# Code search on one Trainium2 core: the add of the chosen codes as an accumulating DMA, four buffers for the gathered rows, a later store

## The chip, the cores and the metric

The kernel runs on one core of a Trainium2 chip. The metric is the device time of one execution in microseconds; less is better. Engines are named PE (matrix), PEld (its weight loads), DVE (vector), ACT (scalar), POOL (GpSimd) and SP (the engine that only issues DMAs); "POOLq" and "SPq" are their sequencers.

## The reference

The input x is (8, 64, 256, 256) in float32. Two layers are added to it, each on a group-normalised copy (32 groups, so two channels to a group):

```
x = x + dct_conv(gn(x), weights1, weights2)   # cosine transform, 64x64 mix of 2 x 32 x 32 modes, transform back
x = x + nearest_code(gn(x), embeddings)       # rows of D = 64 values, K = 1024 codes
def nearest_code(x, e):
    flat = x.reshape(-1, 64)
    distances = sum(flat^2) + sum(e^2) - 2 * flat @ e
    return e.T[argmin(distances, axis=1)]      # the chosen code itself
```

## The kernel before, in words

The work is cut into 256 groups (`NG`), each two channels of one image, kept as a tile `X[:, buf8]` of 128 partitions by 1024 floats, eight of them in turn. The first 0.8 ms of the kernel do the forward transform of all groups (stage A) and the mixing of modes (stage M); both use tiles `Xb` and `Oc`, which nobody touches afterwards. The change is in stage B, which fills the rest: for each group it transforms back and adds x, normalises, searches the best code for each row of 64 values, and adds that code.

A group holds 131072 values, so 2048 rows of 64, and these are 16 steps (`NT`) of 128 rows, one row to a partition. Codes are scored in pairs: in each step PE makes two 128x512 results, the score of the even code and the difference to the odd one (L554), ACT takes the positive part of the difference (`relu`, L723), and DVE adds the two and keeps the maximum (`best`, L929), then finds its place (`find`, L939), which is the number of the pair. POOL then gathers by an indirect DMA (`gather`, L1033) the 128 rows of the pair table: 196 floats each, with both codes, their difference and the difference of their norms. A group later DVE decides between even and odd from the gathered rows: `products` in two halves (L948, at step 5 and 6 of the next group), `sum_products` (L953), ACT's `sum_product`, `choose` (L959, step 13), `settle` in two halves (L964, step 14 and 15). Then `finish` (L1040) on POOL adds the chosen code into X, and SP stores X (`store_y`).

All engines run their own program, in order; the order is written out by hand. Groups are unrolled by eight (`U`), in a loop of 32 passes; each engine branches at the end of a pass. Of POOL's program this is what one group asks: gathers of step 0 to 15, with `inverse_deviation(three)` (L1026) after the gather of step 13, and `finish(before)`, the add of the previous group, after the gather of step 15. Since the gather of step 15 waits for a `find` that runs in step 0 of the next group, the add runs at the start of the next group but one.

The gathered rows lie in `q`, which has two buffers; the gather of step 0 waits until `finish` of two groups before is done (`b_fin`). `best` and `find` have four buffers in flight, and `find` of step 0 waits until the gathers of two groups before have landed.

SP's program for each group r is: turn the normalised halves of group r + 1 by a transposing DMA (`turn_y`) and copy them when they have landed (`copy_yh`), half 0, then half 1; load X of group r + 5 (`load_x`); load its modes (`load_modes`); then store group r - 1 (`store_y`), which waits for `b_fin`.

Of the kernel before, what the change touches and what calls it, by code (L numbers as in the profile page):

```python
# [28 lines left out]
ALU = mybir.AluOpType  # L29
# [8 lines left out]
P = 128  # L38
# [3 lines left out]
U = 8  # L42
NI = NG // U
# [10 lines left out]
D = 64  # L54
K = 1024
NP = K // 2
NT = CG * H * W // D // P
ROW = 3 * D + 4
TA = 8
LOW = (3, 7)  # L60
HT = (slice(0, NT // 2), slice(NT // 2, NT))
# [52 lines left out]
def need(eng, sem, count):  # L114

    if not isinstance(count, int) or count > 0:
        eng.wait_ge(sem, count)


def program(nc, x, w1, w2, emb, c_fh, c_fw, c_ih, c_iw, c_id, c_gm, c_rm, out):  # L120
    spec = nc.dram_tensor("spec", [B, C, MX * MY], F32, kind="Internal").ap()
    mixed = nc.dram_tensor("mixed", [NG, MX, CG * MY], F32, kind="Internal").ap()
    table = nc.dram_tensor("table", [NP, ROW], F32, kind="Internal").ap()
# [8 lines left out]
    with ExitStack() as ctx:  # L132
        def sb(name, shape, dt=F32):
            return ctx.enter_context(nc.sbuf_tensor(name, shape, dt))

        def sem(name):
            return ctx.enter_context(nc.semaphore(name))
# [30 lines left out]
        sc = sb("sc", [P, 9])  # L168
# [23 lines left out]
        def from_arena(*dims):  # L192

            size = int(np.prod(dims))
            taken[0] += size
            assert taken[0] <= 2 * C * CH
            names = "abc"[:len(dims)]
            return arena[:, taken[0] - size:taken[0]].rearrange(
                f"p ({' '.join(names)}) -> p {' '.join(names)}", **dict(zip(names, dims)))

        Xc = sb("Xc", [P, 2, B, CH])
        Xb = sb("Xb", [P, 2, CH, 2 * B])
        Oc = sb("Oc", [P, 2, C, MY])
# [9 lines left out]
        Y = from_arena(4, NT, D)  # L213
# [3 lines left out]
        Fm = from_arena(4, NP)  # L217
        mx = sb("mx", [P, 4])
        idx = sb("idx", [P, 2, NT, 8], U32)
        q = from_arena(2, NT, ROW)  # L220
        prod = from_arena(NT, D)
        dot = sb("dot", [P, NT])
        odd = sb("odd", [P, NT], I32)
# [28 lines left out]
        gath = [sem(f"gath{n}") for n in range(4)]  # L252
        b_inv, b_t, b_conv, b_x1, b_sq, b_st, b_delta2, b_ve, b_rs, b_rr, b_nb = (
            sem("b_" + n) for n in "inv t conv x1 sq st delta2 ve rs rr nb".split())
        b_y, b_yl, b_sc, b_rl, b_ttr, b_mi, b_p, b_red, b_dot, b_sel, b_pr, b_fin = (
            sem("b_" + n) for n in "y yl sc rl ttr mi p red dot sel pr fin".split())
        b_ls = sem("b_ls")
        turned = [[sem(f"turned{h}{n}") for n in range(2)] for h in range(2)]
        t2_in = [[sem(f"t2_in{h}{n}") for n in range(2)] for h in range(2)]
# [1 line left out]
        def hold(eng, name, count):  # L261


            if not isinstance(count, int):
                eng.sem_inc(held[name], 1)
# [5 lines left out]
        def _(sp):  # L271
# [67 lines left out]
            def load_x(g):  # L339
                need(sp, y_out[g.buf8], 16 * g.visit(8))  # L340
                sp.dma_start(X[:, g.buf8].rearrange("p (i f) -> p i f", i=CG), x_g[g.n]).then_inc(x_in[g.buf8], 16)

            def load_modes(g):
                need(sp, b_inv, g.n - 1)
                sp.dma_start(M[:, g.buf2], mixed[g.n]).then_inc(m_in[g.buf2], 16)

            def store_y(g):
                need(sp, b_fin, g.n + 1)
                sp.dma_start(out_g[g.n], X[:, g.buf8].rearrange("p (i f) -> p i f", i=CG)).then_inc(y_out[g.buf8], 16)

            sp.wait_ge(a_h, NG // 2)
# [8 lines left out]
            def turn_y(g, h):  # L360

                need(sp, b_yl, 2 * g.n + h + 1)
                hold(sp, "sp", g.n)
                if h == 0:
                    need(sp, b_sc, NT * (g.n - 1))
                    hold(sp, "sp", g.n)
                sp.dma_start_transpose(t1[:, g.buf2, HT[h]],
                                       YS[:, HT[h]].rearrange("p k f -> p (k f)")).then_inc(turned[h][g.buf2], 16)

            def copy_yh(g, h):  # L370
                need(sp, turned[h][g.buf2], 16 * (g.visit(2) + 1))
                hold(sp, "sp", g.n)
                sp.dma_start(t2[0:D, g.buf2, HT[h]], t1[0:D, g.buf2, HT[h]]).then_inc(t2_in[h][g.buf2], 16)
# [7 lines left out]
            def body(i):  # L381
                for r in range(U):
                    if Group(i, r + 1).exists():
                        for h in range(2):
                            turn_y(Group(i, r + 1), h)
                            copy_yh(Group(i, r + 1), h)
                    if Group(i, r + 5).exists():
                        load_x(Group(i, r + 5))
                    if Group(i, r + 5).exists():
                        load_modes(Group(i, r + 5))  # L390
                    if Group(i, r - 1).exists():
                        store_y(Group(i, r - 1))

            body(0)
            with sp.Fori(1, NI - 1) as i:
                body(i)
            body(NI - 1)
            store_y(Group(NI - 1, U - 1))
            for n in range(U):
                sp.wait_ge(y_out[n], 16 * NI)  # L400

# [378 lines left out]
        def _(dve):  # L780
# [8 lines left out]
            V = nc.vector  # L789
# [152 lines left out]
            def products(g, h):  # L942
                if h == 0:
                    need(dve, gath[g.buf4], 16 * NT * (g.visit(4) + 1))
                else:
                    need(dve, b_dot, TA * g.n)
                hold(dve, "dve", g.n)
                V.tensor_tensor(prod[:, HT[h]], q[:, g.buf2, HT[h], 2 * D:3 * D], Y[:, g.buf4, HT[h]],  # L948
                                ALU.mult).then_inc(b_p, 1)

            def sum_products(g):
# [3 lines left out]
            def choose(g):  # L955
                need(dve, b_red, g.n + 1)
                need(dve, b_dot, TA * (g.n + 1))
                hold(dve, "dve", g.n)
                V.tensor_tensor(odd[:], dot[:], q[:, g.buf2, :, 3 * D], ALU.is_gt).then_inc(b_sel, 1)  # L959

            def settle(g, h):
                need(dve, b_sel, g.n + 1)
                hold(dve, "dve", g.n)
                V.copy_predicated(q[:, g.buf2, HT[h], 0:D], odd[:, HT[h]].unsqueeze(2).broadcast_to([P, NT // 2, D]),  # L964
                                  q[:, g.buf2, HT[h], D:2 * D]).then_inc(b_pr, 1)

            def small_step(g, k, at):

# [37 lines left out]
            for h in range(2):  # L1006
                products(last, h)
            sum_products(last)
            choose(last)
            for h in range(2):  # L1010
                settle(last, h)


        @block.gpsimd
        def _(pool):
            G = nc.gpsimd
            pool.wait_ge(amax_in, 1)
            G.partition_all_reduce(amax, amax0, P, RMAX).then_inc(amax_all, 1)
            pool.wait_ge(s_ve, 1)
            G.tensor_tensor(r_c[:], v_c[:], mhalf[:], ALU.pow).then_inc(s_rstd, 1)  # L1020


            def inverse_deviation(g):
                need(pool, b_ve, g.n + 1)
                need(pool, b_rr, g.n)
                G.tensor_tensor(rs, ve, mhalf[:, 0:1], ALU.pow).then_inc(b_rs, 1)  # L1026

            def gather(g, k):
                need(pool, b_mi, NT * g.n + k + 1)
                if k == 0:  # L1030
                    need(pool, b_fin, g.n - 1)
                hold(pool, "pool", g.n)
                G.indirect_dma_start(out=q[:, g.buf2, k], out_offset=None, in_=table,  # L1033
                                     in_offset=bass.IndirectOffsetOnAxis(ap=idx[:, g.buf2, k, 0:1], axis=0)
                                     ).then_inc(gath[g.buf4], 16)

            def finish(g):
                need(pool, b_pr, 2 * (g.n + 1))
                xg = X[:, g.buf8].rearrange("p (k d) -> p k d", d=D)
                G.tensor_tensor(xg, xg, q[:, g.buf2, :, 0:D], ALU.add).then_inc(b_fin, 1)  # L1040

            def body_b(i):
                for r in range(U):
                    g, before = Group(i, r), Group(i, r - 1)
                    three = Group(i, r + 3)
                    for k in range(NT):
                        gather(g, k)
                        if three.exists() and k == 13:
                            inverse_deviation(three)
                        if before.exists() and k == 15:  # L1050
                            finish(before)

            pool.wait_ge(tab_out, 16)
            inverse_deviation(Group(0, 0))
            inverse_deviation(Group(0, 1))
            inverse_deviation(Group(0, 2))
            body_b(0)
            with pool.Fori(1, NI - 1) as i:
                body_b(i)
            body_b(NI - 1)  # L1060
            finish(Group(NI - 1, U - 1))


# [30 lines left out]
```

## Time and profile before

| | us |
|---|---|
| median of 3 runs (7206.6 to 7208.57) | 7208.31 |
| the profiled execution's own time | 7212.89 |
| span of that execution, first to last instruction | 7210.9 |
| mean granted TensorE clock | 0.956 of full speed |

The times are of whole executions. The profile is of one execution, 4.6 us slower than the median, 2.0 us of which lie outside its span. In the page, the share of an engine is its busy time by the span; issuing a DMA counts as busy on POOL, where it takes POOL's own time, and not on SP. "Idle before" is what an engine waited, with the instruction or DMA that ended the wait; "issue" means that the profile shows no wait for anything.

### The profile page before, as it was taken

Reading aid. Unit: us, or ns where it says so; the run is one execution under the profiler, and the core shown is the slowest. Engines: PE = TensorE matmul, PEld = TensorE weight load, DVE = VectorE, ACT = ScalarE, POOL = GpSimd, SP = SyncE. Lnnn points to the kernel's source line nnn. Section 1 sums busy time; section 2 is a strip of 40 time slices with the busy share of each in tenths; the row PEclk is TensorE's granted clock in tenths of the full one; section 3 lists DMA queues with packets and bytes.
Section 4 is the critical chain, followed back from the end, with each engine's and each line's share of the span. In section 5 each row is a group of like instructions: output and inputs, shape, how many; then the busy total and the mean of one; then the engine's idle time right before and its main releaser. Section 6 shows DMA issues by size and latency. Waiting matters only on the chain. (4 is left out here: it accounts for less than half of the span.)

```text
span 7210.9 us, 142512 instructions
## 1 busy us (share of the span) xinstructions
PE 6465.4 (90%) x25616; PEld 2543.4 (35%) x25616; DVE 6512.0 (90%) x19053; ACT 4720.0 (65%) x12193; POOL 4800.5 (67%) x4614
## 2 busy tenths in 40 slices
PE   7898899999999999899998998998989999899997
PEld 3458333333333333333333333333333333333332
DVE  7771599999999999999999999999999999999998
ACT  2331576677767766667777776767767776777675
POOL 0000377777777777777777777777777777777777
PEclk9998899999999999999999999999999999999999
DMA  7989365665656555656656665556666665666565
GB/s 249 303 279 186 82 144 134 137 144 139 141 137 141 142 137 137 141 136 142 143 139 139 141 142 138 142 138 142 140 141 142 141 140 136 141 141 141 137 140 120
DMA packets 1139144, 1077.66 MB, mean 149 GB/s; under 512 B 702944, under 2 KB 843040, under 8 KB 1138144
## 3 DMA queue, kind: packets, MB, share of 16 engines
q1 hardware_dynamic: 924640, 651.61, 36.0%
q0 software_dynamic: 196608, 411.30, 25.6%
q14 instruction: 712, 5.83, 0.3%
q10 hardware_dynamic: 16896, 4.20, 0.3%
q8 instruction: 288, 4.72, 0.3%
HBM read 722.32 MB, written 143.01 MB: 120 GB/s over the span
## 5 line engine op out<-in xcount | busy, mean ns | idle before, releaser
L1033 POOL DMA_INDIRECT arena<-table,idx x4096 | 4042.6, 987 | 1592.2 <-issue 1157.6
L723 ACT ACTIVATE arena<-bank 128x512 f32<-128x512 f32 x4096 | 2435.0, 595 | 1673.4 <-PE bank L554 1503.9
L554 PE MATMUL bank<-eh,t 128*128 128x512 f16 x8192 | 2516.2, 389 | 576.9 <-DVE mx L929 342.4
L929 DVE CUSTOM_DVE_ANT_0 arena<-bank,arena 128x512 f32<-128x512 f32 x4096 | 2775.4, 678 | 265.6 <-ACT arena L723 217.0
L939 DVE FIND_INDEX8 idx<-mx,arena 128x8 uint32<-128x512 f32 x4096 | 2812.4, 687 | 0.0
L554 PE MATMUL bank<-el,t 67*128 67x512 f16 x8192 | 2504.1, 387 | 0.0
L554 PEld LDWEIGHTS bank<-eh,t 128*128 128x128 f16 x8192 | 590.9, 98 | 2534.1 <-issue 1407.6
L554 PEld LDWEIGHTS bank<-el,t 67*128 67x128 f16 x8192 | 817.4, 100 | 1013.1 <-issue 72.8
L1040 POOL TENSOR_TENSOR X<-X,arena 128x1024 f32<-128x1024 f32 x256 | 605.4, 2365 | 11.1 <-DVE arena L964 5.0
L519 PE MATMUL conv<-iw,Ts 64*128 64x512 f32 x1024 | 586.1, 653 | 0.0
L514 PE MATMUL conv<-X,ident 128*128 128x512 f32 x1024 | 556.4, 625 | 2.4 <-issue 1.8
L533 PE MATMUL bank<-arena,ident 128*128 128x512 f32 x1024 | 550.6, 619 | 6.0 <-ACT arena L703 4.6
L711 ACT ACTIVATE arena<-arena 128x64 f32<-128x64 f32 x2048 | 499.9, 248 | 13.4 <-DVE arena L948 13.4
L855 DVE BATCH_NORM_STATS2 st<-X 128x6 f32<-128x512 f32 x512 | 324.1, 679 | 97.0 <-DMA X<-x 90.9
L948 DVE TENSOR_TENSOR arena<-arena 128x512 f32<-128x512 f32 x512 | 359.3, 702 | 54.4 <-DMA arena<-table,idx 52.5
L711 ACT ACTIVATION_READ_ACCUMULATOR arena<-arena 128x1 f32 x2048 | 397.4, 194 | 0.0
L717 ACT CAST YS<-bank 128x512 f16<-128x512 f32 x512 | 299.6, 585 | 138.5 <-PE bank L534 137.8
L964 DVE COPY_PREDICATED arena<-odd,arena 128x512 f32<-128x512 int32 x512 | 374.9, 733 | 0.0
L939 DVE MATCH_VALUE_LOAD idx<-mx,arena 128x8 f32 x4096 | 354.7, 87 | 0.0
L929 DVE DVE_READ_ACCUMULATOR2_ANT mx<- 128x1 f32 x4096 | 346.3, 85 | 0.0
L1020 POOL TENSOR_TENSOR r_c<-v_c,mhalf 128x8 f32<-128x8 f32 x1 | 1.7, 1692 | 508.9 <-DVE v_c L889 508.9
L1026 POOL TENSOR_TENSOR small<-small,mhalf 128x1 f32<-128x1 f32 x256 | 148.7, 581 | 273.5 <-DVE small L921 269.1
(107 smaller groups left out, 4565.9 us busy)
## 6 DMA issues: line engine op xcount, KB each, us to landing
X<-x SPq DMA_DIRECT2D x512, 512.0 KB, 4.4
y<-X SPq DMA_DIRECT2D x256, 512.0 KB, 3.1
t<-t SPq DMA_DIRECT2D x512, 128.0 KB
arena<-table,idx POOLq DMA_INDIRECT x4096
arena<-w SPq DMA_DIRECT2D x12, 2048.0 KB, 23.0
arena<-w SPq DMA_DIRECT2D x64, 128.0 KB, 3.0
t<-YS SPq DMA_TRANSPOSE x512
spec<-Fs SPq DMA_DIRECT2D x256, 16.0 KB, 3.5
```

The source lines that it names most:

```text
L514: nc.tensor.matmul(conv[:, t].rearrange("p (i w) -> p i w", i=CG), ident[:], xg[:, t], start=True, stop=False)
L519: nc.tensor.matmul(conv[:, t], Ts[:, t * P:(t + 1) * P], iw[:], start=False, stop=True).then_inc(b_conv, 1)
L533: nc.tensor.matmul(low, ident[:], Y[:, g.buf4, HT[h]], start=True, stop=False)
L554: last = nc.tensor.matmul(bank[4 + place(k) % 2 if e else k % 4][:], tile[0:rows, g.buf2, k], codes[0:rows, e], start=rows == P, stop=rows ...
L711: nc.scalar.activation(prod[:, k], prod[:, k], ACT.Identity, accum_out=dot[:, k:k + 1]).then_inc(b_dot, 1)
L723: nc.scalar.activation(R[:, k % 4], bank[4 + place(k) % 2][:], ACT.Relu).then_inc(b_rl, 1)
L929: V.tensor_tensor_reduce(out=Fm[:, k % 4], in0=bank[k % 4][:], in1=R[:, k % 4], scale=1.0, scalar=-3.0e38, op0=ALU.add, op1=ALU.max, accum ...
L939: V.max_index(idx[:, g.buf2, k], mx[:, k % 4:k % 4 + 1].broadcast_to([P, 8]), Fm[:, k % 4]).then_inc(b_mi, 1)
L948: V.tensor_tensor(prod[:, HT[h]], q[:, g.buf2, HT[h], 2 * D:3 * D], Y[:, g.buf4, HT[h]], ALU.mult).then_inc(b_p, 1)
L964: V.copy_predicated(q[:, g.buf2, HT[h], 0:D], odd[:, HT[h]].unsqueeze(2).broadcast_to([P, NT // 2, D]), q[:, g.buf2, HT[h], D:2 * D]).then ...
L1033: G.indirect_dma_start(out=q[:, g.buf2, k], out_offset=None, in_=table, in_offset=bass.IndirectOffsetOnAxis(ap=idx[:, g.buf2, k, 0:1], axis=0)
L1040: G.tensor_tensor(xg, xg, q[:, g.buf2, :, 0:D], ALU.add).then_inc(b_fin, 1)
```

## The change

Three things change. `finish` on POOL becomes a DMA with `accum_op=ALU.add`, issued by POOL, that reads the first 64 floats of each of the 16 gathered rows of a partition (16 runs of 256 bytes) and adds them into the partition's 4096 bytes of X. Its landing raises `b_fin[buf4]` by 16. The gathered rows get four buffers: two as before, and one each in the tiles `Xb` and `Oc`; the gather of step 0 now waits for the add of four groups before. SP's store moves from the end of group r's list, where it stored group r - 1, to a place behind the turned halves and ahead of `load_x`, where it stores group r - 2.

```
-        q = from_arena(2, NT, ROW)
+        q = [from_arena(NT, ROW) for n in range(2)]
+        for kept in (Xb[:].rearrange("p v m b -> p (v m b)"), Oc[:].rearrange("p v o m -> p (v o m)")):
+            q.append(kept[:, 0:NT * ROW].rearrange("p (k w) -> p k w", k=NT))
...
+        b_fin = [sem(f"b_fin{n}") for n in range(4)]
...
             def store_y(g):
-                need(sp, b_fin, g.n + 1)
+                need(sp, b_fin[g.buf4], 16 * (g.visit(4) + 1))
...
                         for h in range(2):
                             turn_y(Group(i, r + 1), h)
                             copy_yh(Group(i, r + 1), h)
+                    if Group(i, r - 2).exists():
+                        store_y(Group(i, r - 2))
                     if Group(i, r + 5).exists():
                         load_x(Group(i, r + 5))
                     if Group(i, r + 5).exists():
                         load_modes(Group(i, r + 5))
-                    if Group(i, r - 1).exists():
-                        store_y(Group(i, r - 1))
...
-            store_y(Group(NI - 1, U - 1))
+            for r in range(U - 2, U):
+                store_y(Group(NI - 1, r))
...
             def gather(g, k):
                 need(pool, b_mi, NT * g.n + k + 1)
                 if k == 0:
-                    need(pool, b_fin, g.n - 1)
+                    need(pool, b_fin[g.buf4], 16 * g.visit(4))
                 hold(pool, "pool", g.n)
-                G.indirect_dma_start(out=q[:, g.buf2, k], out_offset=None, in_=table,
+                G.indirect_dma_start(out=q[g.buf4][:, k], out_offset=None, in_=table,
...
             def finish(g):
                 need(pool, b_pr, 2 * (g.n + 1))
+                hold(pool, "pool", g.n)
                 xg = X[:, g.buf8].rearrange("p (k d) -> p k d", d=D)
-                G.tensor_tensor(xg, xg, q[:, g.buf2, :, 0:D], ALU.add).then_inc(b_fin, 1)
+                G.dma_start(xg, q[g.buf4][:, :, 0:D], accum_op=ALU.add).then_inc(b_fin[g.buf4], 16)
```

`products`, `choose` and `settle` read the same rows under the new name `q[g.buf4]`.

## Rows read from the trace of the kernel before

**Rows 1.** The page, its first lines: the span, and each engine's busy time.
```profile
span 7210.9 us, 142512 instructions
...
PE 6465.4 (90%) x25616; PEld 2543.4 (35%) x25616; DVE 6512.0 (90%) x19053; ACT 4720.0 (65%) x12193; POOL 4800.5 (67%) x4614
```

**Rows 2.** The page's groups: line, engine, operation, count | busy us, mean ns | idle before.
```profile
L1033 POOL DMA_INDIRECT arena<-table,idx x4096 | 4042.6, 987 | 1592.2 <-issue 1157.6
...
L929 DVE CUSTOM_DVE_ANT_0 arena<-bank,arena 128x512 f32<-128x512 f32 x4096 | 2775.4, 678 | 265.6 <-ACT arena L723 217.0
L939 DVE FIND_INDEX8 idx<-mx,arena 128x8 uint32<-128x512 f32 x4096 | 2812.4, 687 | 0.0
...
L1040 POOL TENSOR_TENSOR X<-X,arena 128x1024 f32<-128x1024 f32 x256 | 605.4, 2365 | 11.1 <-DVE arena L964 5.0
...
L948 DVE TENSOR_TENSOR arena<-arena 128x512 f32<-128x512 f32 x512 | 359.3, 702 | 54.4 <-DMA arena<-table,idx 52.5
```

**Rows 3.** Windows: length, then busy us of each engine, granted clock, DMA share, GB/s.
```profile
3841.80:3865.40 23.60, 22.30 (x84) 8.16 (x83) 23.60 (x73) 17.68 (x47) 17.37 (x17) 1.00 0.54 142
3937.30:3961.30 24.00, 22.12 (x83) 8.10 (x82) 23.76 (x73) 17.67 (x47) 18.69 (x18) 1.00 0.70 146
3801.60:4001.10 199.50, 180.82 (x656) 65.97 (x656) 190.17 (x568) 141.29 (x369) 148.00 (x143) 0.97 0.59 140
```

**Rows 4.** Timeline of POOL about one group: start us, duration us, [idle before].
```profile
3912.28 0.96 POOL L1033 DMA_INDIRECT arena<-table,idx  x1 [0.80 <-issue]
...
3930.08 0.58 POOL L1026 TENSOR_TENSOR small<-small,mhalf 128x1 f32<-128x1 f32 x1
...
3932.13 0.95 POOL L1033 DMA_INDIRECT arena<-table,idx  x1 [0.30 <-issue]
3933.10 2.37 POOL L1040 TENSOR_TENSOR X<-X,arena 128x1024 f32<-128x1024 f32 x1
3936.27 0.97 POOL L1033 DMA_INDIRECT arena<-table,idx  x1 [0.80 <-issue]
```

**Rows 5.** Timeline of DVE: the first `best` of five groups.
```profile
3801.63 0.69 DVE L929 CUSTOM_DVE_ANT_0 arena<-bank,arena 128x512 f32<-128x512 f32 x1 [2.72 <-ACT arena L723]
...
3832.29 0.67 DVE L929 CUSTOM_DVE_ANT_0 arena<-bank,arena 128x512 f32<-128x512 f32 x1
...
3855.83 0.68 DVE L929 CUSTOM_DVE_ANT_0 arena<-bank,arena 128x512 f32<-128x512 f32 x1
...
3927.34 0.67 DVE L929 CUSTOM_DVE_ANT_0 arena<-bank,arena 128x512 f32<-128x512 f32 x1
...
3951.27 0.68 DVE L929 CUSTOM_DVE_ANT_0 arena<-bank,arena 128x512 f32<-128x512 f32 x1
```

**Rows 6.** `products`: L948 over one pass, ns min/median/max; then one first half.
```profile
L948 DVE TENSOR_TENSOR arena<-arena x16: 665/674/864, 3816.1 to 3985.1; 128x512 f32<-128x512 f32 x16
...
3935.24 0.79 DVE L948 TENSOR_TENSOR arena<-arena 128x512 f32<-128x512 f32 x1 [0.20 <-DMA arena<-table,idx]
```

**Rows 7.** Timeline of SP's issues in the same group.
```profile
3936.39 1.48 SPq L367 DMA_TRANSPOSE t<-YS  x1
3942.02 0.47 SPq L373 DMA_DIRECT2D t<-t  x1
3942.69 1.65 SPq L367 DMA_TRANSPOSE t<-YS  x1
3948.22 0.46 SPq L373 DMA_DIRECT2D t<-t  x1
```

**Rows 8.** The page's DMA queues: packets, MB, share of 16 engines' span.
```profile
q1 hardware_dynamic: 924640, 651.61, 36.0%
q0 software_dynamic: 196608, 411.30, 25.6%
```

**Rows 9.** Timeline of the tail: the last group's products and its add.
```profile
7195.23 1.40 DVE L948 TENSOR_TENSOR arena<-arena 128x512 f32<-128x512 f32 x2 [6.62 <-DMA arena<-table,idx]
...
7200.42 2.34 POOL L1040 TENSOR_TENSOR X<-X,arena 128x1024 f32<-128x1024 f32 x1 [4.96 <-DVE arena L964]
```

More of the change, by code:

```diff
@@ L254, in program @@
             sem("b_" + n) for n in "inv t conv x1 sq st delta2 ve rs rr nb".split())
-        b_y, b_yl, b_sc, b_rl, b_ttr, b_mi, b_p, b_red, b_dot, b_sel, b_pr, b_fin = (
-            sem("b_" + n) for n in "y yl sc rl ttr mi p red dot sel pr fin".split())
+        b_y, b_yl, b_sc, b_rl, b_ttr, b_mi, b_p, b_red, b_dot, b_sel, b_pr = (
+            sem("b_" + n) for n in "y yl sc rl ttr mi p red dot sel pr".split())
+        b_fin = [sem(f"b_fin{n}") for n in range(4)]
         b_ls = sem("b_ls")
@@ L947, in products @@
                 hold(dve, "dve", g.n)
-                V.tensor_tensor(prod[:, HT[h]], q[:, g.buf2, HT[h], 2 * D:3 * D], Y[:, g.buf4, HT[h]],
+                V.tensor_tensor(prod[:, HT[h]], q[g.buf4][:, HT[h], 2 * D:3 * D], Y[:, g.buf4, HT[h]],
                                 ALU.mult).then_inc(b_p, 1)
@@ L958, in choose @@
                 hold(dve, "dve", g.n)
-                V.tensor_tensor(odd[:], dot[:], q[:, g.buf2, :, 3 * D], ALU.is_gt).then_inc(b_sel, 1)
+                V.tensor_tensor(odd[:], dot[:], q[g.buf4][:, :, 3 * D], ALU.is_gt).then_inc(b_sel, 1)
             def settle(g, h):
@@ L963, in settle @@
                 hold(dve, "dve", g.n)
-                V.copy_predicated(q[:, g.buf2, HT[h], 0:D], odd[:, HT[h]].unsqueeze(2).broadcast_to([P, NT // 2, D]),
-                                  q[:, g.buf2, HT[h], D:2 * D]).then_inc(b_pr, 1)
+                V.copy_predicated(q[g.buf4][:, HT[h], 0:D], odd[:, HT[h]].unsqueeze(2).broadcast_to([P, NT // 2, D]),
+                                  q[g.buf4][:, HT[h], D:2 * D]).then_inc(b_pr, 1)
             def small_step(g, k, at):
```

## The prediction

> **What bounds the kernel now.** I began with the page's busy times: PE and DVE both stand at 90%, POOL at 67% [rows 1]. The groups show what POOL's 67% hides: "idle before" of its gathers is 1592 us, and 1158 of that is "issue", time in which it waited for nothing [rows 2]. So I went to POOL's timeline. There a gather takes 0.95 us and 0.30 us pass before it, 1.25 us a step, with no wait in them. The add takes 2.37 us and is followed by 0.80 us instead of 0.30: from the gather before it (3932.13) to the one behind it (3936.27) are 4.14 us, so the add costs POOL 4.14 - 1.25 = 2.89 us net. From the first gather of this group to that of the next are 3936.27 - 3912.28 = 23.99 us, all of it used [rows 4]. POOL is full, at 67% busy.
>
> DVE's own pace comes from a group in which it waits for nothing. In the window 3841.8 to 3865.4 it is busy 23.60 of 23.60 us [rows 3], and the first `best` of this group and of the next are 3855.83 - 3832.29 = 23.54 us apart. In a later group of the same pass they are 3951.27 - 3927.34 = 23.93 us apart [rows 5]. There `products` waits for the last gather: that gather is issued until 3933.08, its rows land 2.16 us later, at 3935.24, and DVE had been idle 0.20 us [rows 4, 6]. So two engines stand within 2% of each other, DVE at 23.54 and POOL at 24.0. After the branch at the end of a pass DVE stands idle for some time for PE and ACT (2.72 us before one `best` [rows 5]; 199.50 - 190.17 = 9.3 us in the whole pass [rows 3]). In it POOL catches up, and then it falls behind by about half a microsecond a group, until DVE waits for it.
>
> What POOL costs the kernel is then what DVE loses at `products`: 52.5 us of waits for gathers [rows 2], and the stretch of `products` itself, mean 702 ns where one that isn't disturbed takes about 670 (665 the shortest) [rows 2, 6]: 512 x 0.032 = 16 us. The stretch has its place: the product that began at 3935.24 ended at 3936.03, 0.56 us after the add ended (3935.47), where an undisturbed one takes 0.67 us in all [rows 4, 6]. It stood until POOL's add was over. By the Trainium skill (SBUF — State Buffer, "Who interferes with whom") a DVE instruction with two SBUF inputs blocks against a GpSimd one that reads SBUF; the trace agrees, 0.79 us against a median of 0.67. Together 52.5 + 16 = 69 us. That is all a faster POOL can give in stage B, 1.0%: DVE follows at once.
>
> **The change, part by part.** *The add leaves POOL's datapath.* 256 x 2.89 us net go, and 256 issues of a DMA come. Let P be what such an issue takes, gap included. POOL's cycle becomes 24.0 - 2.89 + P. The whole 69 us are won if the cycle is at or under DVE's 23.54, so for P up to about 2.5 us. At 2.89 nothing is won. Above, a pass of eight groups becomes longer by 6 times the excess (six adds lie between the first gather of a pass and the last one on which DVE waits; the one in the branch's pause is covered as long as the excess is small): 6 x 32 = 192 us for each microsecond of P.
>
> The trace has no DMA of this kind. From below: it is at least a gather's step, 1.25 us [rows 4]; a gather is 128 runs. The new DMA has 128 x 16 = 2048 runs of 256 bytes, and reads no indices. From above: a POOL instruction on one column takes 0.58 us [rows 4], so of the gather's 0.95 at most 0.37 us belong to its 128 runs, 2.9 ns each; 2048 of them are 5.9 us, with 0.58 and 0.30 this makes 6.8 us. Should all of a gather's time belong to its runs, it would be 16 x 1.25 = 20 us, which I leave to the tail beyond the range. The bounds lie on both sides of 2.89. The row nearest in the number of runs is SP's transposing issue, about 1024 runs (8 steps of 128 rows) in 1.3 to 1.65 us against 0.47 us for a copy of 64 rows: some 1 ns a run [rows 7], from another generator; 2048 runs would be 2 us, and with the gap 2.3. I take a P of 1.3 to 2.5 us, and hold it with little more than even weight against all above.
>
> The Trainium skill (DMA: Bandwidth & Descriptors, "Anatomy of one DMA — SWDGE (gpsimd) path") says of descriptor generation that "You can emit a lot of descriptors before the incremental cost shows up". By that P would be the lower bound, 1.25 us, and the sum the same 69 us; no run so far shows it.
>
> *The transfer itself.* 512 KB are read from the gathered rows and 512 KB from X, and 512 KB written. The DMA engines are busy 0.59 of a pass [rows 3], 0.59 x 24.9 = 14.7 us a group. A packet on SP's queue takes on average 0.36 x 16 x 7210.9 / 924640 = 45 ns [rows 8]; most of those are small. 2048 / 16 = 128 runs on each engine at 25 to 90 ns (half a packet to two) are 3 to 11.5 us, so the share goes to 0.72 to 1.05. I take about 6 us, 0.83: it lands some 8 to 10 us after the issue, which nothing needs sooner. The gather that DVE waits for stands ahead of it in POOL's order.
>
> *Four buffers.* They cost no instruction, and the added `hold` no time that counts. The gather of step 0 now waits for an add issued two groups earlier, some 45 us; cover is ample. Were the landing that late, every later step would be late; I see nothing for it.
>
> *The store.* Three issues change places on SP: the store of a group now goes behind `copy_yh` of half 1 (3948.22 in this group [rows 7]), 15 us after the add's issue, and in front of `load_x` and `load_modes`. Behind it wait the X of group r + 5, wanted two groups later, and modes wanted a group later. The X buffer that `load_x` waits for was stored one body earlier, a full 24 us. Nothing to pay. With the old place the store would wait for the landing ahead of `turn_y`, and that is avoided.
>
> *The tail.* The last add takes 2.34 us [rows 9]; in its place stand an issue and a landing, 1.3 + some 6 us, so 5 us more. The last products wait less: DVE was idle 6.62 us before them [rows 9] because POOL was behind, by some 3 us that go. Net +2 us.
>
> Sum, for P up to 2.5 us: 7212.9 - 69 + 2 = 7146 for the profiled execution. It was 4.6 us above the median of the runs shown, so 7141 for a median.
>
> **The rivals.**
>
> *POOL's issue is dearer than the add (slower).* It decides at P = 2.9 us. For it: 2048 runs against 128. Against it: much of a gather's time is fixed, and its steps are regular. At 4.4 us (middle of the bounds on a log scale) 1.5 x 192 = 288 us come on top, 7500. At 6.8 us 3.9 x 192 = 749, so 7957. At 20 us every one of the 256 adds counts, about 17 x 256 = 4400, over 11000.
>
> *The turned halves come late (slower).* SP's two halves follow each other by landings: turn half 0 at 3936.39, land by 3942.0, turn half 1 at 3942.69, land by 3948.2 [rows 7]; ACT overwrites their source for the next group, whose first `best` runs at 3951.27 [rows 5]. The slack to DVE is 3 us. The accumulating DMA runs from about 3934 to 3943, right beside the first half. If it holds that back by 5 us, DVE loses 2 us in seven of eight groups: 2 x 224 = 448, so about 7590. For it: the DMA engines are at 0.70 in one such group already, over 0.54 in another [rows 3]. Against it: the halves' own packets are few.
>
> *The DMA engines are full (slower).* It decides at (24.9 - 14.7) = 10 us for the added transfer, 80 ns a run. At 90 ns the group takes 26.2 us, 1.3 x 256 = 330 us more, 7540.
>
> *The exchange is even.* P between 2.8 and 3.0 us, POOL's cycle as now: 7195 to 7225.
>
> **How the numbers follow.** A difference under 0.2%, 14 us, can't be told from none here. Chances: P up to 2.8 with nothing late, 0.46 (of this 0.02 for a part gain too small to tell, counted as same); even exchange 0.06; POOL's issue dearer 0.33, of which 0.20 up to 7500, 0.06 from there to 7950, and 0.07 beyond; late halves 0.10; full DMA engines 0.05, of which some lie beyond 7950. So faster 0.44, same 0.08, slower 0.48. The likeliest single case is the gain, and its time is 7141; its own range is 7130 to 7185. The slower cases together hold a little more, but spread over hundreds of microseconds. The range for 8 in 10 goes from 7128 (the whole 69 us and a tail that costs nothing, with 10 us to spare) to 7957, the upper bound of P; about 0.1 lies above it, little below.
>
> **What the profile after would show.** Right: the step from the gather before POOL's DMA to the one after it under 3.75 us (1.25 + 2.5); no `products` that waits for a gather outside the first groups of a pass; their mean at 0.67 us; the first `best` of neighbouring groups 23.54 us apart in seven of eight groups; a DMA share near 0.83. Wrong: that step at 4.1 us or more, and `products` idle before it in every group (POOL's issue); ACT's YS (L698) or PE's L554 waiting for t<-YS or t<-t (late halves); a DMA share near 1 (full engines); SP's store waiting beyond the branch of a group. My prediction hangs above all on P, which no row of before shows.

## The result and the profile after

| | before | after |
|---|---|---|
| median of 4 runs, us | 7208.44 (7206.6 to 7214.43) | 7133.36 (7110.83 to 7156.06) |
| ratio, 95% interval | | 0.9894 (0.9862 to 0.9927) |
| profiled execution, its span | 7212.89, 7210.9 | 7130.59, 7128.5 |

The changed kernel is 1.1% faster, 75 us by the medians. The forecast was 7141 us. Its four runs lie 45 us apart and those of the kernel before 8; but over the 8 to 13 runs that the experiments have of the kernel before, these too spread by 17 to 33 us.

The page after, for the busy times, the slices and the queues:

```profile
span 7128.5 us, 142900 instructions
...
PE 6430.6 (90%) x25616; PEld 2529.7 (35%) x25616; DVE 6490.3 (91%) x19053; ACT 4723.3 (66%) x12193; POOL 4818.1 (68%) x4614
...
DMA  7989599999999999999999999999999999999999
...
q0 software_dynamic: 724992, 545.54, 51.7%
q1 hardware_dynamic: 924640, 651.61, 40.9%
```

The busy times are those of before [rows 1] within 0.6%. Of the 82 us that the span lost, DVE's own busy time gave 22 (6512.0 - 6490.3), and 60 were time in which it stood idle. What stands out is the row of the DMA engines, at nine tenths or more in every slice of stage B, and POOL's queue, which went from 196608 packets to 724992 [rows 8]. The second number is 528384 more, 2064 a group: a packet for each run of 256 bytes, and 16.

POOL's timeline around its new DMA:

```profile
3930.40 0.95 POOL L1037 DMA_INDIRECT Xb<-table,idx  x1 [0.31 <-issue]
3931.34 2.27 POOL L1045 DMA_DIRECT2D X<-arena  x1
3933.92 1.07 POOL L1037 DMA_INDIRECT Oc<-table,idx  x1 [0.30 <-issue]
```

From gather to gather are now 3933.92 - 3930.40 = 3.52 us, where there were 4.14 [rows 4]. Look at the parts: issuing the DMA takes 2.27 us, hardly less than the add's 2.37. What went is the gap behind it, 0.30 instead of 0.80.

DVE's groups: busy, mean ns, and idle before with what ended it.

```profile
L933 DVE CUSTOM_DVE_ANT_0 arena<-bank,arena 128x512 f32<-128x512 f32 x4096 | 2790.7, 681 | 245.6 <-ACT arena L727 160.1 <-issue 83.6
...
L952 DVE TENSOR_TENSOR arena<-arena 128x512 f32<-128x512 f32 x256 | 174.0, 680 | 5.4 <-DMA arena<-table,idx 4.7
...
L952 DVE TENSOR_TENSOR arena<-Xb,arena 128x512 f32<-128x512 f32 x128 | 87.1, 680 | 2.2 <-DMA Xb<-table,idx 1.9
L952 DVE TENSOR_TENSOR arena<-Oc,arena 128x512 f32<-128x512 f32 x128 | 86.7, 678 | 5.1 <-DMA Oc<-table,idx 5.1
```

`products` waits 12.7 us in all, where it waited 54.4 [rows 2], and one takes 680 ns instead of 702. In the windows the DMA share is the last number but one:

```profile
3801.60:4001.10 199.50, 181.70 (x662) 66.25 (x660) 191.10 (x576) 142.16 (x374) 151.62 (x146) 0.97 0.94 163
1000.00:7000.00 6000.00, 5488.48 (x19940) 2006.05 (x19938) 5753.38 (x17263) 4284.10 (x11184) 4572.61 (x4377) 0.97 0.95 163
```

0.94 stands against 0.59 [rows 3]. Where the time went is best seen in the lengths of the groups, by their place r in a pass of eight: the distance from the first `best` of a group to that of the next, a mean over the 32 passes, worked out from the trace's 256 first `best`s. Two kernels of the experiments stand with them.

| us | r = 0 | 1 | 2 | 3 | 4 | 5 | 6 | 7 | r = 1 to 6 over 6 x 23.54 | r = 0 and 7 over 2 x 23.54 |
|---|---|---|---|---|---|---|---|---|---|---|
| before | 30.06 | 23.57 | 23.56 | 23.71 | 23.88 | 24.09 | 24.29 | 26.48 | 1.86 | 9.46 |
| after | 28.85 | 23.71 | 23.54 | 23.62 | 23.66 | 23.62 | 23.54 | 26.57 | 0.45 | 8.34 |
| four buffers alone | 29.90 | 23.55 | 23.54 | 23.55 | 23.60 | 23.54 | 23.54 | 25.87 | 0.08 | 8.69 |
| later store alone | 29.13 | 23.61 | 23.59 | 23.67 | 23.89 | 24.11 | 24.19 | 25.74 | 1.82 | 7.79 |

Most of the drift in groups 3 to 6, POOL falling behind DVE, is gone: 1.41 x 32 = 45 us. The groups on both sides of the branch give another 1.12 x 32 = 36 us, which the prediction didn't count. Together that is 81 of the 82 us of the span. The table has one execution of each kernel, and its last column varies from branch to branch, so small differences in it are not sharp.

### The profile page after: what moved, and what is told of

Same layout as the page of the kernel before. It is cut to its first block and busy times, and to the rows that moved or that the text cites. A ratio compares the mean times of both kernels' runs of the same rounds, so it can differ in the third digit from the quotient of the medians.

```text
span 7128.5 us, 142900 instructions
## 1 busy us (share of the span) xinstructions
PE 6430.6 (90%) x25616; PEld 2529.7 (35%) x25616; DVE 6490.3 (91%) x19053; ACT 4723.3 (66%) x12193; POOL 4818.1 (68%) x4614
## 3 DMA queue, kind: packets, MB, share of 16 engines
q0 software_dynamic: 724992, 545.54, 51.7%
q1 hardware_dynamic: 924640, 651.61, 40.9%
## 5 line engine op out<-in xcount | busy, mean ns | idle before, releaser
L1037 POOL DMA_INDIRECT arena<-table,idx x2048 | 2044.3, 998 | 796.5 <-issue 540.5
L1037 POOL DMA_INDIRECT Oc<-table,idx x1024 | 1021.6, 998 | 393.8 <-issue 260.0
L1037 POOL DMA_INDIRECT Xb<-table,idx x1024 | 1019.1, 995 | 304.0 <-issue 263.5
L715 ACT ACTIVATE arena<-arena 128x64 f32<-128x64 f32 x2048 | 499.4, 248 | 11.3 <-DVE arena L952 11.3
L943 DVE MATCH_VALUE_LOAD idx<-mx,arena 128x8 f32 x4096 | 371.1, 91 | 0.0
L933 DVE DVE_READ_ACCUMULATOR2_ANT mx<- 128x1 f32 x4096 | 362.2, 88 | 0.0
L707 ACT ACTIVATE arena<-X,small 128x1024 f32<-128x1024 f32 x256 | 315.8, 1234 | 0.0
```

The lines of the kernel that those rows point to most:

```text
L707: nc.scalar.activation(Y[:, g.buf4], xg, ACT.Identity, bias=nb, scale=rr).then_inc(b_y, 1)
L715: nc.scalar.activation(prod[:, k], prod[:, k], ACT.Identity, accum_out=dot[:, k:k + 1]).then_inc(b_dot, 1)
L933: V.tensor_tensor_reduce(out=Fm[:, k % 4], in0=bank[k % 4][:], in1=R[:, k % 4], scale=1.0, scalar=-3.0e38, op0=ALU.add, op1=ALU.max, accum ...
L943: V.max_index(idx[:, g.buf2, k], mx[:, k % 4:k % 4 + 1].broadcast_to([P, 8]), Fm[:, k % 4]).then_inc(b_mi, 1)
L1037: G.indirect_dma_start(out=q[g.buf4][:, k], out_offset=None, in_=table, in_offset=bass.IndirectOffsetOnAxis(ap=idx[:, g.buf2, k, 0:1], axis=0)
```

## The experiments

Medians in us; "before" is the kernel before on the same chip, 7205 to 7214 us each time. First, each part of the change by itself.

**Everything but the DMA.** The four buffers and the later store stay, the add is POOL's again (and the counts of `b_fin` go by 1 in place of 16):

```
-                G.dma_start(xg, q[g.buf4][:, :, 0:D], accum_op=ALU.add).then_inc(b_fin[g.buf4], 16)
+                G.tensor_tensor(xg, xg, q[g.buf4][:, :, 0:D], ALU.add).then_inc(b_fin[g.buf4], 1)
```

> The change without its DMA: four buffers and the later store, the add stays on POOL. If the gain is POOL's time (2.27 us net for the DMA's issue against 2.89 for the add, read from the two traces), nothing is won: 7200 to 7215 us, the step around the add still 4.14 us. If the buffers or the store's place carry the gain, about 7135 us.

7100.5, ratio 0.9854 (0.9832 to 0.9876): faster than the changed kernel, not slower. POOL's timeline says why:

```profile
3923.16 0.95 POOL L1037 DMA_INDIRECT Xb<-table,idx  x1 [0.30 <-issue]
3924.14 2.36 POOL L1045 TENSOR_TENSOR X<-X,arena 128x1024 f32<-128x1024 f32 x1
3926.66 0.97 POOL L1037 DMA_INDIRECT Oc<-table,idx  x1 [0.16 <-issue]
```

The add takes what it always took, but the gap behind it is 0.16 us and not 0.80, and the step is 3.50 us, the same as with the DMA. With two buffers the gather behind the add waits for that very add, which has just ended. With four it waits for one issued two groups earlier. The 0.64 us are the price of waiting for one's own last result, which the profile calls "issue".

**No add at all.** As above, but `finish` issues nothing, so the kernel leaves out the second layer's sum; the store waits for `settle`.

> The changed kernel with the second add left out (x of the second layer isn't added to; the store waits for settle). POOL then has 2.27 us a group less to do and the DMA share falls back to about 0.65. If the vector engine's 23.54 us a group is the floor that the changed kernel already stands on, 7120 to 7135 us, hardly less than the changed kernel. If the nearly full DMA engines (share 0.95) or POOL still cost something, clearly less, 7080 or under.

7093.9, 0.9848 (0.9825 to 0.987). Taking all of the add's work away gives 7 us beyond the first experiment, within the intervals of the two: from there a faster POOL is worth next to nothing.

**Four buffers alone**, with the store in its old place, and **the later store alone**, with two buffers. The second one's edit, in SP's program of the kernel before:

```
+                    if Group(i, r - 2).exists():
+                        store_y(Group(i, r - 2))
                     if Group(i, r + 5).exists():
                         load_x(Group(i, r + 5))
...
-                    if Group(i, r - 1).exists():
-                        store_y(Group(i, r - 1))
```

> The kernel before with four buffers for the gathered rows and nothing else: the add on POOL, the store in its old place. With all but the DMA (7100) POOL's step around the add fell from 4.14 to 3.50 us, since the gather behind it no longer waits for the add (0.16 us of gap for 0.80). If the buffers carry that alone, the step is 3.50 us here too and at least the 69 us of waits at products go: 7136 us; 7100 if they also bring what is won at the branch of a pass. If the store's place carries it, 7205.

> The kernel before with the later store alone, two buffers. The step around the add stays 4.14 us and products wait as before. If the store's place makes the branch of a pass shorter (some 30 us in all), 7175 us; if it does nothing, 7205.

Four buffers: 7124.7, 0.9875 (0.9859 to 0.9892). Later store: 7152.26, 0.9914 (0.9899 to 0.9929). So each part of the change that issues no new instruction pays by itself, 90 and 62 us by the medians. Their traces show that they do it in different places. With the buffers alone, POOL:

```profile
3919.98 0.95 POOL L1036 DMA_INDIRECT Xb<-table,idx  x1 [0.30 <-issue]
3920.96 2.37 POOL L1044 TENSOR_TENSOR X<-X,arena 128x1024 f32<-128x1024 f32 x1
3923.48 0.96 POOL L1036 DMA_INDIRECT Oc<-table,idx  x1 [0.16 <-issue]
```

With the later store alone, POOL, and DVE's groups:

```profile
3927.22 0.95 POOL L1034 DMA_INDIRECT arena<-table,idx  x1 [0.30 <-issue]
3928.20 2.37 POOL L1041 TENSOR_TENSOR X<-X,arena 128x1024 f32<-128x1024 f32 x1
3931.37 0.97 POOL L1034 DMA_INDIRECT arena<-table,idx  x1 [0.80 <-issue]
```
```profile
L930 DVE CUSTOM_DVE_ANT_0 arena<-bank,arena 128x512 f32<-128x512 f32 x4096 | 2756.4, 673 | 205.1 <-ACT arena L724 198.5 <-issue 3.7 <-DVE idx L940 0.9
...
L949 DVE TENSOR_TENSOR arena<-arena 128x512 f32<-128x512 f32 x512 | 354.3, 692 | 64.0 <-DMA arena<-table,idx 61.9
```

The buffers cut POOL's step, and the drift in groups 1 to 6 goes from 1.86 to 0.08 us a pass (table), 57 us. The store leaves step and drift as they were, and `products` still waits, 64.0 us; what it shortens is the idle time of `best`, 205.1 us against 265.6 [rows 2], and that lies at the branch: 9.46 - 7.79 = 1.67 us a pass, 53 us. Before, SP stood at the store for POOL's add, 240 times and 2773.7 us between 1000 and 7000 by the waits of its queue, with the next turned halves behind it. With the store behind them they come earlier: half 1 is copied 10.2 us ahead of the first `best` that needs it (median of r = 3, worked out from the trace), where it was 5.6 us.

**The slope.** Two small operations more for POOL in each group, at steps 3 and 6, in the kernel before and in the one after:

```
+                        if k in (3,6):
+                            at = (3,6).index(k)
+                            need(pool, b_ex, 2 * (g.n - 1) + at + 1)
+                            G.tensor_tensor(extra[:, at:at + 1], mhalf[:, 0:1], mhalf[:, 0:1], ALU.mult).then_inc(b_ex, 1)
```

> The kernel before with two more small POOL instructions a group, each some 0.47 us net. By the sum of the prediction (192 us for each microsecond of POOL's time above its 2.89 us) 0.94 x 192 = 180 us more, 7390 us; with all eight adds of a pass in it 0.94 x 256 = 240, 7450. If POOL is not the engine that sets the pace, 7208.

> The changed kernel with the same two instructions. POOL's excess over the kernel before is 2.27 + 0.94 - 2.89 = 0.32 us, so 7208 + 0.32 x 192 = 7270 us. If the gain comes from anything else than POOL's time (port, buffers), the two instructions cost little and it stays near 7140.

7226.94, 1.0025 (1.0012 to 1.0038), and 7132.11, 0.989 (0.9868 to 0.9913). The dose was too small to test much: such an operation takes 0.20 us, and as it replaces part of the gap, the steps around the two grew by some 0.2 us a group. The signs are as expected, 21 us by the medians on the kernel whose POOL is full, nothing on the one with room. So it was done again on the kernel before with a power (`ALU.pow`, of a column of `avg`) in place of the multiplication:

> As e3, whose two extra instructions turned out to cost POOL only about 0.1 us each, but with two that raise to a power, as L1026 does (0.58 us, 0.47 net): 0.94 us a group. At the 192 us for each microsecond of the prediction 7385 us; at the slope that e3 shows (21 us for some 0.2) 7305; if POOL doesn't set the pace, 7205.

7378.98, 1.0224 (1.0207 to 1.0242), 165 us more by the medians. The dose was larger than the 0.94 us that was expected. POOL's timeline around one of the two powers:

```profile
3927.82 0.96 POOL L1035 DMA_INDIRECT arena<-table,idx  x1 [0.30 <-issue]
3928.80 0.57 POOL L1053 TENSOR_TENSOR extra<-avg,mhalf 128x1 f32<-128x1 f32 x1
3929.55 1.00 POOL L1035 DMA_INDIRECT arena<-table,idx  x1 [0.17 <-issue]
3930.85 0.95 POOL L1035 DMA_INDIRECT arena<-table,idx  x1 [0.31 <-issue]
```

The two steps take 3930.85 - 3927.82 = 3.03 us for 2.50 without, so a power costs 0.53 us, and some gathers last longer too. By the whole cycle, from a group's first gather to the next one's (medians at r = 5 and 6, worked out from the traces), POOL went from 23.96 to 25.20 us: 1.24 us a group. That makes 165 / 1.24 = 133 us for each microsecond of POOL. The groups grow by 1.62, 1.42, 1.28 and 0.92 us at r = 3 to 6 and by 0.2 us or less at r = 0 to 2: about four groups of a pass pay the excess, and POOL's lead after the branch covers the first three. DVE's waits at `products` went from 54.4 [rows 2] to 231.5 us:

```profile
L950 DVE TENSOR_TENSOR arena<-arena 128x512 f32<-128x512 f32 x512 | 370.4, 724 | 231.5 <-DMA arena<-table,idx 230.8
```

**What the DMA costs POOL and the engines.** A plain copy in its place (`accum_op` left out), and an accumulating one for half of the rows:

```
-                G.dma_start(xg, q[g.buf4][:, :, 0:D], accum_op=ALU.add).then_inc(b_fin[g.buf4], 16)
+                G.dma_start(xg[:, 0:NT // 2], q[g.buf4][:, 0:NT // 2, 0:D], accum_op=ALU.add).then_inc(b_fin[g.buf4], 16)
```

> The changed kernel with a plain copy in place of the accumulating DMA (the second layer's x is overwritten, not added to). If the reading of X makes half of the transfer's cost, its packets take some 30 ns for 57, the DMA share falls from 0.95 to about 0.8, POOL's issue from 2.27 to about 1.7 us, and the time to 7100 or 7115. If 256-byte runs cost what they cost whatever is done with them, all stays: 0.95, 2.27, 7133.

> The changed kernel with an accumulating DMA over 8 of the 16 rows of a partition (half of the second add is left out). If each run of 256 bytes is a packet of 57 ns, the DMA share falls from 0.95 to about 0.79; if POOL writes descriptors run by run, its issue falls from 2.27 to about 1.4 us. If the load of the DMA engines is what makes the branch of a pass longer (5.0 us from the last best of a pass to the first of the next at a share of 0.95, 4.3 at 0.71, 3.5 at 0.61), it is about 4.3 us and the time 7115 us; if the load doesn't matter, 5.0 and 7133.

Copy 7125.78, 0.9877 (0.9859 to 0.9895); half of the rows 7136.97, 0.9896 (0.9882 to 0.991). The copy's group, queue and window:

```profile
L1045 POOL DMA_DIRECT2D X<-arena x128 | 156.4, 1222 | 0.4
```
```profile
q0 software_dynamic: 233472, 545.54, 34.8%
```
```profile
1000.00:7000.00 6000.00, 5519.43 (x19937) 2013.80 (x19936) 5749.88 (x17260) 4284.03 (x11183) 4361.99 (x4376) 0.97 0.71 163
```

The half's:

```profile
L1045 POOL DMA_DIRECT2D X<-arena x128 | 221.0, 1727 | 0.4
```

The copy moves the same 545.54 MB on that queue, but in (233472 - 196608) / 256 = 144 packets a group and not 2064, and POOL issues it in 1.22 us; the whole accumulating one takes 2.26 us and half of it 1.73. Between 1024 and 2048 accumulated runs that is 0.53 us, 0.52 ns a run, over a start of 1.2 us. And yet three lengths of POOL's DMA, 1.22, 1.73 and 2.26 us, give times within each other's intervals: POOL has room in all of them.

**The landing exposed.** First the accumulating DMA with two buffers, where the gather of step 0 waits for the landing of the DMA issued just ahead of it; then with four buffers and the store in its old place. One run each.

> The changed kernel with two buffers as before: the gather behind the accumulating DMA must wait for its landing. That takes 10.2 us from the issue's start by the packets, for 2.57 us of the step now, so POOL's group grows by 7.6 us to about 31 us and the time to 8700 or 8900 us. If the landing were short (3 us, as a store's), 7250.

> The changed kernel with the store in its old place, ahead of the next turned halves. SP then waits for the landing (some 14.7 us into a group), and the two halves take 13 us more, so they end at 27.7 us where the next group's normalised rows want their source at 23.5: some 4 to 5 us more a group, 8200 to 8400 us. If SP has slack enough, 7133 to 7170.

With two buffers 8935.85. POOL's timeline:

```profile
4028.22 0.96 POOL L1036 DMA_INDIRECT arena<-table,idx  x1 [0.30 <-issue]
4029.18 2.25 POOL L1044 DMA_DIRECT2D X<-arena  x1
4039.62 1.08 POOL L1036 DMA_INDIRECT arena<-table,idx  x1 [8.18 <-DVE idx L941]
```

4039.62 - 4029.18 = 10.4 us from the issue's start to the gather that waits for the landed sum; over all groups the median is 11.1 us (9.4 to 12.8). The row names DVE's `find`, but the `find` of that step had ended a median of 22 us before the gather began, over all groups; it is the landing that POOL waits for. With the store in the old place 7756.16. SP's waits in 2000 to 7000 (in all, times, longest) and its timeline:

```profile
SPq L352 <- DMA X<-arena: 1165.9, 92, 17.5
SPq L352 <- DMA X<-Oc: 707.3, 46, 19.9
SPq L352 <- DMA X<-Xb: 514.0, 46, 17.1
```
```profile
3943.19 0.54 SPq L348 DMA_DIRECT2D M<-mixed  x1
3955.02 0.40 SPq L352 DMA_DIRECT2D y<-X  x1
3955.78 1.45 SPq L370 DMA_TRANSPOSE t<-YS  x1
```

SP has nothing issued for 11.3 us, and `turn_y` of the next group stands behind that.

**Passes of 16 groups.** The branch was left as the largest idle stretch. This is the first experiment (add on POOL, four buffers, later store) with stage B unrolled twice as far, on all five engines:

```
-                for r in range(U):
+                for r in range(2 * U):
...
-            with sp.Fori(1, NI - 1) as i:
-                body(i)
-            body(NI - 1)
+            with sp.Fori(1, NI // 2 - 1) as i:
+                body(2 * i)
+            body(NI - 2)
```

> Four buffers and the later store with the add on POOL (e1), and stage B unrolled by 16 groups, so that it branches 15 times for 31. A branch costs e1 some 8.3 us over two plain groups (25.2 + 30.3 - 2 x 23.55). Halved, 16 x 8.3 = 133 us less: 6970 us. If the pause belongs to something that comes every eight groups whatever the loop (the X tiles, the prefetch of instructions), 7100.

6927.98, 0.9615 (0.9602 to 0.9629): 3.8% faster than before, and 2.9% faster than the changed kernel. DVE's `best` in the page:

```profile
L933 DVE CUSTOM_DVE_ANT_0 arena<-bank,arena 128x512 f32<-128x512 f32 x4096 | 2746.6, 671 | 67.8 <-ACT arena L727 54.0
```

The idle time of `best` is 67.8 us, where the first experiment had 229.2. By the lengths of the groups a branch now costs 25.88 + 25.71 - 2 x 23.54 = 4.5 us, against 7.7 there, and there are 15 seams between bodies in place of 31: 31 x 7.74 - 15 x 4.51 = 172 us, and 7100.5 - 6927.98 = 172.5 were measured. It is not something that comes every eight groups: the eighth and ninth group of the longer body take 23.54 and 23.56 us.

The first and the last body stand outside the loop, so the seam into the loop and the seam out of it have no jump back. The traces tell them apart: in the first experiment these two seams cost 0.06 and 0.01 us, the other 29 a mean of 8.4, and here 13 cost a mean of 5.2. What else comes with the jump is TensorE's granted clock. Windows of the first experiment, before the seam at 4141.7, at it, and at the next seam:

```profile
4134.10:4138.30 4.20, 0.00 (x0) 0.00 (x0) 4.20 (x13) 0.60 (x1) 3.29 (x4) 0.99 0.86 198
4138.30:4145.00 6.70, 5.60 (x11) 1.82 (x12) 3.83 (x13) 3.45 (x4) 4.13 (x6) 0.50 0.23 58
4145.00:4161.00 16.00, 15.91 (x60) 6.02 (x59) 13.17 (x37) 10.35 (x25) 9.50 (x9) 1.00 0.41 93
4332.90:4349.90 17.00, 15.13 (x28) 5.18 (x29) 7.40 (x22) 5.50 (x8) 9.50 (x9) 0.50 0.19 46
```

PE stands still first, 4.6 us; then the granted clock falls to 0.50, the 1.2 GHz level, and two of PE's matmuls take 1.03 us where they take 0.60 at 1.00. PE was busy 15.09 of the 16 us before, so DVE waits for it until the clock is back. The low stretch is 6.8 us long at the first of these seams and 17.1 at the second; half of the difference is 5.1 us of PE's time, and the seams cost 6.46 and 11.51 us, 5.05 apart. Over this execution 9 seams have a low stretch of 6.8 us and cost a mean of 6.6, 11 have 10.2 and cost 7.3, 8 have 17.1 and cost 11.5, one has 20.5 and costs 12.6; the two without a jump have none. With passes of 16 all 13 have 6.8 us. So most of what a branch is cheaper there goes with the shorter low clock: 6.8 us against a mean of 11.4, and half of that difference is 2.3 of the 3.2 us. Why its stretch is short in one case and long in another no run here shows.

## Why the prediction was right, and the step of it that failed

The time came out 8 us under the forecast, inside its own range of 7130 to 7185. That it came so close is in part luck. The gain was put down to the DMA, which gives none; of the 69 us at `products` the drift gave 45; and the 36 us at the branch were not in the sum.

**What POOL costs the kernel: right in kind, somewhat high in size.** The waits and the stretch at `products` were put at 69 us, and the condition at a step under 3.75 us. The step became 3.52, the waits 12.7 us, and the groups in the middle of a pass 23.54 to 23.71. By the groups 45 us were won there, and 57 by the four buffers alone. The kernel without any add bounds what is to be had on POOL, and it is 7 us beyond the first experiment. The slope was forecast at 192 us per microsecond, six groups of a pass; it measured 133, about four groups. That the time with the two powers still met its expectation (7378.98 for 7385) is luck: the dose was a third larger than assumed, the slope a third smaller. Rows of before that were enough for this: DVE without a wait in one window, and the drift of half a microsecond in another [rows 3, 5].

**The step that failed: "Four buffers. They cost no instruction, and the added `hold` no time that counts."** They were costed at nothing, and the whole 4.14 - 1.25 = 2.89 us was put down to the add. 0.64 of it was the wait of the next gather on the add's own end. That is the whole gain in POOL's step, 4.14 to 3.52 us: four buffers alone have a step of 3923.48 - 3919.98 = 3.50 us, and the drift ends. The price P of the DMA was put at 1.3 to 2.5 us with the gap and is 3.52 - 1.25 = 2.27, but the add's price with four buffers is 3.50 - 1.25 = 2.25. On POOL, removing the add was an even exchange. The row that could have told is the first of [rows 4], the gather with 0.80 us before it that the prediction read only as part of the add's cost: it stood among gathers with 0.30 us, and among them the gather of step 0 alone waits on `b_fin`.

**Its companion: "Nothing to pay" for the store.** It was meant as neither gain nor loss, and taken by itself the move is worth 62 us, 53 of them at the branch by the groups. The prediction took the idle time there (9.3 us in one pass) as given. Buffers and store together save 105 us, not 90 + 62: both shorten the branch, by 0.77 and 1.67 us, and together by 9.46 - 7.74 = 1.72.

**The DMA gives some of it back.** Without it 7100.5, with it 7133.36: 33 us. By the groups it is 0.6 us at the branch (8.34 against 7.74) and 0.26 us between, in each pass, 27 us. The intervals of the two ratios overlap a little, and runs of the changed kernel spread by 45 us, so the size is not sharp. The sign is: the runs of the changed kernel (7110.83 to 7156.06) and those with two small operations more (7118.68 to 7137.63) all lie above the slowest of the first experiment (7110.36). This was not in the sum, which had the DMA as the source of the gain.

**The cost of issuing.** The estimate of some 1 ns a run from SP's queue was twice what it is, 0.52. The Trainium skill (DMA: Bandwidth & Descriptors, "Anatomy of one DMA — SWDGE (gpsimd) path") says that many descriptors can be emitted before it shows. By that P would have been 1.25 us. For the accumulating DMA it doesn't hold, 2.26 us of issue for 2048 runs and 1.73 for 1024, and the measurement decides. The plain copy, 1.22 us, is no test of it, as it went out as 144 packets.

**The transfer.** Forecast 6 us and a share of 0.83; it is 0.95 by the window. A share near 1 was named as a sign of being slower; it came, and the kernel was still faster. The queue's share gives the time of a packet: (0.517 x 16 x 7128.5 - 0.256 x 16 x 7210.9) / 528384 = 55.7 ns, within the 25 to 90 assumed, and 2064 of them on 16 engines are 7.2 us. The trace's packets of 256 bytes on that queue have a mean of 56.8 ns (56.0 with half of the rows). The rest of the growth is on other queues, 40.9% of 7128.5 us on q1 where 36.0% were [rows 8]: the packets of 256 bytes there took 26.4 ns before and 35.4 after, but 26.3 beside half of the rows. The landing, 10.4 to 11.1 us with two buffers, lies above the "8 to 10". The copy counts the same bytes and leaves the share at 0.71, so the bytes written are not what fills the engines; whether it is the packet for each run or the adding itself, these runs don't separate.

**The late halves.** The rival was half right. The DMA does hold them back: in the timeline of SP's queue after, the second turn takes 3.29 us to issue where it took 1.65 [rows 7], and 3944.83 - 3937.05 = 7.78 us pass until its copy, where it was 5.53 (medians over the groups: 2.5 us for 1.3, and 8.2 for 4.6).

```profile
3930.49 1.26 SPq L370 DMA_TRANSPOSE t<-YS  x1
3936.14 0.50 SPq L376 DMA_DIRECT2D t<-t  x1
3937.05 3.29 SPq L370 DMA_TRANSPOSE t<-YS  x1
3944.83 0.46 SPq L376 DMA_DIRECT2D t<-t  x1
```

Half 1 is copied 6.1 us ahead of the first `best` in the changed kernel (median of r = 3), 9.9 us with the add on POOL, 5.6 us before. The store's move had made 4 us of room, and the DMA used them up. With the store in its old place there is no such room, SP waits for the landing, and the kernel takes 7756 us. So the reason given for the move, that the old place would wait for the landing ahead of `turn_y`, is shown; its size was expected at 8200 to 8400 and was overstated.

**The port.** `products` takes 680 ns instead of 702, and 669 to 673 with the add on POOL and four buffers. Counted from the traces, 108 of the 512 `products` of the kernel before ran while POOL's add was under way, at a mean of 806 ns against 674 for the rest; in the first experiment one did. It is thus not the add's reading that matters but whether the two meet; with POOL no longer late, they don't. The last 8 ns are not the DMA's: in the kernel with two small operations more, which has the same DMA, `products` takes 672 ns and `best` 673. In the traces of the kernels before and after `best` stands at 678 and 681; why these two are longer is open.

## What to carry to other kernels

Price each part of a change alone, those that issue nothing too: a second set of buffers removed a wait of 0.64 us on the engine's own last result, and that was the gain which the replaced operation was given credit for. Before an operation is moved to a DMA, compare what the issue takes of the same engine (here 2.26 us against 2.36), and what its packets do to the queues. When an extra load is used to measure a slope, read the dose from the trace: here it was 1.24 us and not 0.94. When the loops' bodies are hand-ordered and full, look at their branch, and at the granted clock behind it: here unrolling twice as far gave 172 us, where buffers and store together gave 105.

## What the runs showed of the hardware that was not expected

- An accumulating DMA went out as one packet for each 256-byte run, some 56 ns each, and with two buffers had landed 10.4 us after its issue began (median 11.1). A plain copy of the same 2048 runs took 16 + 128 packets, and about half of POOL's time.
- A branch cost 7.7 to 9.5 us of DVE's time in a pass of eight groups (by the table's last column). At each jump back of the first experiment PE stood still for some microseconds, and the granted clock fell to 0.50 from 1.2 to 4.6 us after it had stopped, for 6.8 to 20.5 us; at the two seams without a jump neither is seen. At one branch of the changed kernel PE stood still twice, the second time for 3.51 us in which it waited for nothing that the profile shows:

```profile
4147.52 0.96 PE L558 MATMUL bank<-eh,t 128*128 128x512 f16 x2 [3.59 <-DVE mx L933]
...
4152.85 1.01 PE L558 MATMUL bank<-eh,t 128*128 128x512 f16 x2 [3.51 <-issue]
```

At the same branch of the first experiment the second pause is 0.71 us and has a releaser:

```profile
4141.29 1.01 PE L558 MATMUL bank<-eh,t 128*128 128x512 f16 x2 [0.71 <-ACT arena L727]
```

- What sets the length of PE's pauses, and with them that of the low clock, is open. The cost of the branch is 7.7 to 7.8 us a pass with the add on POOL or none and the later store (with two buffers as with four), 8.7 with four buffers and the old store, 9.5 with both as before, and with a DMA from POOL 8.3 (all rows; 8.8 with two small operations more), 8.6 (plain copy) and 9.1 (half of the rows). It follows neither the DMA share (0.95, 0.71, 0.75) nor the length of the issue, nor how early the turned halves come: with the plain copy half 1 is 9.6 us ahead. The instruction queues' packets of 8 and 16 KB gather around a branch: at the one of the first experiment near 4141.7 us 10 of them start from 15 us before to 5 us after the first `best`, and at the seam into the loop 3. So a fetch that PE waits for, and that other transfers slow, is what I would suspect; no run here tells it apart from others.
